# Cross-attention and mixture of experts on one core: each half of the heads on 64 array rows of its own, another order of the turn, register reads moved into the steps

## What is computed

```python
# x: (16, 112, 256), ctx: (16, 375, 256), mask: (16, 375)
q, k, v = (split_heads(layernorm(x) @ Wq.T + bq), split_heads(ctx @ Wk.T + bk), split_heads(ctx @ Wv.T + bv))
scores = where(mask == 0, -1e9, einsum('bhqd,bhkd->bhqk', q, k) / 4)
x = x + (merge(softmax(scores) @ v) @ Wo.T + bo)
flat = layernorm(x).reshape(1792, 256)
w, idx = top_k(softmax(flat @ router_w), 2);  w = w / w.sum()
h = silu(einsum('td,edf->etf', flat, w1));  y = einsum('etf,efd->etd', h, w2)
out = x + sum of w * y over the two chosen experts
```

## Time and profile before

| | us |
|---|---|
| median of 3 runs | 551.58 |
| the runs | 549.52, 551.58, 842.05 |
| the profiled execution, its own time | 552.8 |
| its span, first to last instruction | 550.6 |
| TensorE busy | 436.2 |
| VectorE busy | 349.6 |
| ScalarE busy | 261.3 |
| GpSimd busy | 191.4 |

### The profile page before, as it was taken

The page is one execution under the profiler, slowest core; times in us unless marked ns, Lnnn a source line. Parts: engine busy times, 40 slices in busy tenths (PEclk is TensorE's granted clock), DMA queues, the critical chain, the costliest instruction groups (busy, mean ns, idle before and its releaser), DMA issues.

```text
span 550.6 us, 10586 instructions
## 1 busy us (share of the span) xinstructions
PE 436.2 (79%) x4151; PEld 388.1 (70%) x4151; DVE 349.6 (63%) x743; ACT 261.3 (47%) x338; POOL 191.4 (35%) x162
## 2 busy tenths in 40 slices
PE   2557887999999999999998749322789999999810
PEld 2445666888888888888876648222689999999810
DVE  3676574777777777777773396524276667766617
ACT  3322054555565556655555204000487888788600
POOL 7371251222212222212200420002537778787420
PEclk9996698999999999999999787655699999999965
DMA  7979679899989999999634397000212222222148
GB/s 187 198 186 239 216 102 147 138 147 146 146 137 145 140 150 136 147 145 150 104 40 137 115 395 254 1 1 16 79 40 87 87 81 84 88 87 87 39 158 280
DMA packets 62624, 72.41 MB, mean 132 GB/s; under 512 B 19520, under 2 KB 57824, under 8 KB 62576
## 3 DMA queue, kind: packets, MB, share of 16 engines
q1 hardware_dynamic: 50240, 50.50, 50.7%
q0 software_dynamic: 4032, 11.02, 5.9%
q10 hardware_dynamic: 8304, 10.23, 5.3%
HBM read 37.95 MB, written 15.06 MB: 96 GB/s over the span
## 4 chain that ended last, share of the span: by engine, by line
PE 70%; DVE 11%; issue 8%; DMA 4%; ACT 3%; ACTq 2%; POOL 1%; SPq 1%; POOLq 0%; DVEq 0%
PE ps L1248 38%; PE ps L1298 10%; PE ps L1313 8%; PE ps L1327 7%; ACTq L827 2%; DMA y_back<-y_rows 2%; PE ps L1519 2%; DVE k_f L851 2%; DVE neg_max L867 1%; PE ps L1340 1%; SPq L472 1%; DVE x_rows_sb L914 1%; PE ps L1469 1%; ACT probs L667 1%; PE ps L1348 1%
## 5 line engine op out<-in xcount | busy, mean ns | idle before, releaser
L867 DVE TENSOR_REDUCE neg_max<-ps 112x1 f32<-112x376 f32 x256 | 132.9, 546 | 48.2 <-PE ps L1298 44.3
L667 ACT ACTIVATE probs<-ps 125x1344 f32<-125x1344 f32 x64 | 82.7, 1292 | 57.7 <-PE ps L1313 54.9
L1298 PE MATMUL ps<-k_stack,q_stack 98*112 98x376 f32 x256 | 89.5, 390 | 13.7 <-issue 8.6
L603 POOL DMA_INDIRECT rows<-xn_rows,token_of_row x42 | 50.2, 1195 | 76.7 <-DVE token_of_row L1125 61.5
L1298 PEld LDWEIGHTS ps<-k_stack,q_stack 98*112 98x112 f32 x256 | 42.0, 180 | 32.1 <-DVE neg_max L867 20.8
L611 POOL DMA_INDIRECT y_rows<-y_out,slot_of_row x42 | 47.9, 1140 | 33.8 <-ACT y_out L800 20.5
L502 POOL TENSOR_TENSOR k_lo<-k_f,k_hi 128x752 fp32r<-128x752 f32 x16 | 28.6, 1790 | 83.8 <-ACT k_hi L641 81.3
L493 POOL TENSOR_TENSOR ctx_lo<-ctx_raw,ctx_hi 128x752 fp32r<-128x752 f32 x16 | 28.7, 1795 | 76.9 <-ACT ctx_hi L634 76.9
L1313 PE MATMUL ps<-q_stack,k_stack 100*125 100x224 f32 x384 | 53.6, 275 | 2.1 <-ACT probs L667 1.3
L1313 PEld LDWEIGHTS ps<-q_stack,k_stack 100*125 100x125 f32 x384 | 50.1, 189 | 2.8 <-ACT probs L667 1.8
L1248 PE MATMUL ps<-w_hi,h_hi 128*128 128x256 f32 x168 | 49.0, 292 | 3.1 <-issue 1.6
(11 more groups left out here) (189 smaller groups left out, 992.4 us busy)
## 6 DMA issues: line engine op xcount, KB each, us to landing
k_stack<-k_hi SPq DMA_DIRECT2D x64, 188.0 KB, 6.4
w_all<-w ACTq DMA_DIRECT2D x16, 512.0 KB, 8.6
k_stack<-k_lo SPq DMA_DIRECT2D x32, 188.0 KB, 8.9
ctx_raw<-ctx_t SPq DMA_DIRECT2D x32, 187.5 KB, 8.7
q_stack<-q_scratch SPq DMA_DIRECT2D x32, 168.0 KB
q_scratch<-q_hi SPq DMA_DIRECT2D x16, 224.0 KB, 3.0
y_back<-y_rows SPq DMA_DIRECT2D x14, 256.0 KB, 5.4
keep<-keep_scratch SPq DMA_DIRECT2D x16, 188.0 KB, 8.9
```

The lines of the kernel that those rows point to most:

```text
L603: pool.indirect_dma_start(rows[t.ring][:, a, :], None, xn_rows, row_of(token_i, t, a))\
L667: act.activation(pf[j % 2][:, :, :], ps[0:CT, BK_ST:BK_ST + KT, 0:4 * S], ACT.Exp).then_inc(pf_ready, 1)
L867: dve.tensor_reduce(neg_max[:, s:s + 1], ps[0:S, BK_MAX + s % 2, 0:CP], AX.X, ALU.max, negate=True).then_inc(max_read, 1)
L1298: pe.matmul(ps[0:S, BK_MAX + a, 0:CP], qs[b.ring][0:R_MAX, q, S * a:S * (a + 1)], ks[b.ring][0:R_MAX, q, :], start=True, stop=True).then_i ...
```

## The change

- **Rows.** Each of the two heads of a stack gets 64 array rows of its own: head q in rows 0 to 51, head q + 8 in rows 64 to 115, each with its own mask and maximum rows. The query stack has one column block of 112 and no zeros. Every score matmul names its tile of the array: 64 rows by 128 columns, at row 0 or at row 64. A quad takes 12 matmuls of 112 columns where it took 6 of 224, alternately on the two halves, to different PSUM banks (`score_home`), with one wait on its own semaphore (`even_scored`) where the second half comes to a bank that the first half wrote.
- **Layout.** In a stack the dimension is now first and the part second: the three parts of a dimension lie in neighbouring rows, so one key transfer of 16 rows writes every third row of 48 instead of 16 neighbours. `q_scratch` is laid out likewise. The mask rows are sent twice, once per half.
- **The keep mask** (which keys count) is loaded as bytes in two transfers for all batches; it was 188 KB in each turn. The stacks' constant rows take 5 fills on GpSimd, not 8.
- **Order.** The lists of a turn on TensorE, ScalarE and VectorE are rearranged, a third home for the context's parts is added (`ctx_home`), and the key projection is cut into pieces of 3 matmuls that stand between heads 10 and 14.
- **Registers.** The reads of the expert numbers move into the steps, one per step and engine.

The diff, cut to what matters here:

```diff
-R_MASK, R_MAX, ROWS = 96, 98, 100
+HALF_ROWS = 64
+R_MASK, R_MAX, ROWS = 48, 50, 52
...
+def ctx_home(n):
+    return n if n < 2 else (0, 2, 1)[(n - 2) % 3]
+def score_home(k3, q, a):
+    at = 2 * k3 + q + 6 * a
+    return at // 4, at % 4
...
         qf = sb("q_f32", [P, KD, SG])
...
+        ch.append(sb("ctx_hi2", [P, KD, CP], F32R))
...
+        assert cursor["at"] <= queries_end, "the third context lies where the queries' low parts were"
         cursor["at"] = queries_end
...
         cursor["at"] = attn_start
...
+            def load_keep(part, batches):
+                sp.dma_start(keep[:, batches, :].rearrange("p b n -> p (b n)"),
+                             keep_scratch[batches, :].rearrange("(a b) n -> a (b n)", a=1)
+                             .to_broadcast([P, (batches.stop - batches.start) * CP])).then_inc(keep_in[part], 16)
...
-                    sp.dma_start(qs[b.ring][row:row + PARTS * DK, :, S * a:S * (a + 1)].bitcast(F32),
-                                 q_scratch[a, :, :, S * b.n:S * (b.n + 1)]
-                                 .rearrange("c (d q) n -> (c d) q n", q=HALF)).then_inc(q_stacked[b.ring], 16)
-                sp.dma_start(ks[b.ring][R_MASK:ROWS, :, :].bitcast(F32),
-                             mask_scratch[b.n:b.n + 1, :, :].rearrange("a p n -> p a n")
-                             .to_broadcast([4, HALF, CP])).then_inc(q_stacked[b.ring], 16)
+                    row = HALF_ROWS * a
+                    sp.dma_start(qs[b.ring][row:row + R_MASK, :, :].bitcast(F32),
+                                 q_scratch[a, :, :, :, S * b.n:S * (b.n + 1)].rearrange("d c q n -> (d c) q n"))\
+                        .then_inc(q_stacked[b.ring], 16)
+                    sp.dma_start(ks[b.ring][row + R_MASK:row + ROWS, :, :].bitcast(F32),
+                                 mask_scratch[b.n:b.n + 1, :, :].rearrange("a p n -> p a n")
+                                 .to_broadcast([4, HALF, CP])).then_inc(q_stacked[b.ring], 16)
...
-                        row = DK * (PARTS * a + c)
-                        sp.dma_start(ks[b.ring][row:row + DK, :, :].bitcast(F32), src[:, a, :].bitcast(F32))\
-                            .then_inc(k_stacked[b.ring], 16)
+                        row = HALF_ROWS * a
+                        sp.dma_start(ks[b.ring][row + c:row + R_MASK:PARTS, :, :].bitcast(F32),
+                                     src[:, a, :].bitcast(F32)).then_inc(k_stacked[b.ring], 16)
...
-            fills = [(qs[0][0:R_MASK, :, :], 0.0), (qs[0][R_MASK:ROWS, :, :], 1.0), (vx[0][:, :, :, DK:VC], 1.0),
-                     (qs[1][0:R_MASK, :, :], 0.0), (qs[1][R_MASK:ROWS, :, :], 1.0), (vx[1][:, :, :, DK:VC], 1.0),
-                     (qs[2][0:R_MASK, :, :], 0.0), (qs[2][R_MASK:ROWS, :, :], 1.0)]
+            fills = [(qs[0][:, :, :], 1.0), (vx[0][:, :, :, DK:VC], 1.0), (qs[1][:, :, :], 1.0),
+                     (vx[1][:, :, :, DK:VC], 1.0), (qs[2][:, :, :], 1.0)]
...
+                elif early(b, 3):
+                    act.wait_ge(vproj_done, 2)
+                elif early(b, 4):
+                    for p in range(2):
+                        act.wait_ge(q_written[p], 96 * NG // 2)
                 else:
-                    act.wait_ge(vproj_done, 2 * (b.n - 1))
-                act.copy(ch[b.par][:, :, :], c_raw[b.par][:, :, :]).then_inc(ch_ready, 1)
+                    act.wait_ge(vproj_done, 2 * (b.n - 2))
+                act.copy(ch[ctx_home(b.n)][:, :, :], c_raw[b.par][:, :, :]).then_inc(ch_ready, 1)
...
+                if has(b.after(3)):
+                    ctx_high(b.after(3))
+                if has(after):
+                    values(after, True)
                 if has(b):
                     exps(b, 0)
                 if has(after):
                     values(after, False)
-                if has(before):
-                    out_copy(before)
                 if has(b):
                     exps(b, 1)
-                if has(after):
-                    values(after, True)
-                if has(b.after(3)):
-                    ctx_high(b.after(3))
                 if has(b):
                     exps(b, 2)
                 if has(before):
...
+            experts = []
             def w1_high(t):
...
-            experts = [act.value_load(expert_of[0:1, n:n + 1], min_val=0, max_val=E - 1) for n in range(STEPS)]
...
                 if has(before):
                     normalise(before)
                 if has(after):
-                    max_rows(after)
+                    maxima(after, range(8, H))
                 if has(b.after(3)):
                     keys(b.after(3), 0)
+                if has(after):
+                    max_rows(after)
                 if has(before):
...
-            dve.wait_ge(table_ready, 1)
...
+                if KD - 1 in halves:
+                    last.then_inc(kproj_done, 1)
...
+                    else:
+                        pe.wait_ge(vx_ready, 2 * b.n)
+                elif k3 == 2:
...
                         pe.wait_ge(an_ready, b.n - 2)
...
                     a, q = s % 2, s // 2
-                    pe.matmul(ps[0:S, BK_MAX + a, 0:CP], qs[b.ring][0:R_MAX, q, S * a:S * (a + 1)],
-                              ks[b.ring][0:R_MAX, q, :], start=True, stop=True).then_inc(smax_done, 1)
+                    row = HALF_ROWS * a
+                    pe.matmul(ps[0:S, BK_MAX + a, 0:CP], qs[b.ring][row:row + R_MAX, q, :],
+                              ks[b.ring][row:row + R_MAX, q, :], start=True, stop=True, tile_position=(row, 0))\
...
-                for k3 in range(KT):
-                    for q in range(2):
-                        last = pe.matmul(ps[0:CT, BK_ST + k3, 2 * S * q:2 * S * (q + 1)],
-                                         ks[b.ring][0:ROWS, 2 * j + q, k3 * CT:(k3 + 1) * CT],
-                                         qs[b.ring][0:ROWS, 2 * j + q, :], start=True, stop=True)
+                for even, odd in zip((4, 5, 0, 1, 2, 3), (2, 3, 4, 5, 0, 1)):
+                    for a, n in enumerate((even, odd)):
+                        row, k3, q = HALF_ROWS * a, n // 2, n % 2
+                        bank, at = score_home(k3, q, a)
+                        if a == 1 and n == 0:
+                            pe.wait_ge(even_scored, QUADS * b.n + j + 1)
+                        last = pe.matmul(ps[0:CT, BK_ST + bank, S * at:S * (at + 1)],
+                                         ks[b.ring][row:row + ROWS, 2 * j + q, k3 * CT:(k3 + 1) * CT],
+                                         qs[b.ring][row:row + ROWS, 2 * j + q, :], start=True, stop=True,
+                                         tile_position=(row, 0))
+                        if a == 0 and n == 5:
+                            last.then_inc(even_scored, 1)
                 last.then_inc(st_done, 1)
...
+                def keys(t, *halves):
+                    if has(b.after(3)):
+                        project_keys(b.after(3), t, halves)
+                values(0)
                 heads(0, 1)
-                values(0)
-                heads(2)
                 outputs(before, 2)
-                heads(3, 4)
+                outputs(before, 3)
+                heads(2, 3)
+                values(2)
+                heads(4, 5)
                 scores(0)
-                heads(5)
+                heads(6)
+                if has(before):
+                    out_transpose(before)
+                heads(7)
                 values(1)
-                heads(6)
-                outputs(before, 3)
-                heads(7, 8)
+                heads(8, 9)
                 scores(1)
-                heads(9)
-                values(2)
+                outputs(b, 0)
                 heads(10)
-                outputs(b, 0)
-                heads(11, 12)
+                keys(0, 0)
+                heads(11)
+                keys(0, 1)
+                heads(12)
                 scores(2)
                 heads(13)
-                if has(before):
-                    out_transpose(before)
+                keys(1, 0)
                 heads(14, 15)
                 outputs(b, 1)
+                scores(3)
+                if has(before):
+                    attn_transpose(before)
                 if has(after):
                     max_transpose(after)
-                if has(b.after(3)):
-                    project_keys(b.after(3), 0)
-                if has(before):
-                    attn_transpose(before)
-                scores(3)
-                if has(b.after(3)):
-                    project_keys(b.after(3), 1)
+                keys(1, 1)
```

130 lines of the change are left out of this document (71 added, 59 removed).

## The result

The changed kernel takes **561.3 us** (median of 4 runs, 559.4 to 562.3) against 551.0 us, a ratio of 1.019 with an interval of 1.015 to 1.024. The forecast was 537 us, with a range of 516 to 561. It came out slower than before, though the register reads are gone from the chain.

The account below looks back on a forecast made before the run. TensorE was taken as the bound (70% of the chain), VectorE next. From the profiled 552.8 us, registers -13.6, attention turns +2 and transfers -3.5 gave 537.7, less 1.2 for the median: 537 us, range 516 to 561.

Parts of the forecast that it names:

- Registers, -13.6: Between attention and experts: 21 VectorE register reads leave the chain, -13.6 us, and cost nothing inside the steps.
- Keys before values and joined outputs, -1.30 per turn: Attention turn: -0.94 us as values no longer wait for VectorE's key read, -0.36 from fewer output blocks on column strips.
- waits for maxima: 0: Attention turn: TensorE's waits for VectorE's maxima, 0.08 us where a head follows a quad, stay about as they are: 0.
- Changes of tiling, 0.1 each: Attention turn: 14 places where TensorE goes between 64-row tiles and whole array, 0.1 us each, +1.4 per turn.
- Heads side by side, -0.15: Attention turn: two head score matmuls at once pay only for heads 0 and 1, -0.15 us, bounds 0 and -0.3.
- even_scored: Score quads: TensorE's wait for its own matmul inside every quad, 0.05 us per quad, +0.2 per turn.
- Quads, 0: Score quads: twelve matmuls of 112 columns take the 0.65 us of six of 224, as loads on both halves overlap.
- Transfers, -3.5: Start of the attention: third batch's wait for key stacks shrinks by 2.9 us, plus 0.6 for the clock; bounds 0 and -4.
- The last two turns at nothing: End of the attention: the last two turns, whose chain runs over scores and exponentials in both orders, change by nothing.
- every change costs 0.18: Rival, chance 0.2: each of 14 tiling changes per turn costs the column strips' 0.18 us, 17 us more in all, 554 us.
- Row tiles change for nothing: Rival, chance 0.27: tiling changes in the attention cost nothing, a turn is 14.0 us, 16 us below the forecast, 521 us.
- the halves load in turn: Rival, chance 0.12: weight loads of a quad's two halves do not overlap, +0.65 us per quad, 39 us, 576 us.

Follow-up runs that it names:

- before_regs: The kernel before with only the register reads of both engines moved into the experts' steps; 539.6 us, ratio 0.978.
- full_rows: The changed kernel with the scores on the whole array again instead of row tiles, all else kept; 528.4 us, ratio 0.961.
- full_early_max: full_rows with VectorE's low parts of the output and router weights moved behind the first turn's maxima; 527.9 us.
- regs_ahead: The changed kernel with its registers read in one go ahead of the steps, as before; 578.8 us in one run.
- fewer_changes: The changed kernel with 10 instead of 14 changes between row tiles and whole array per turn; 556.1 us, ratio 1.006.
- after_early_max: The changed kernel with VectorE's low parts of the output and router weights moved behind the first turn's maxima; 558.7 us, median of ten runs.
- before_tiles: regs_layout with the scores on two tiles of 64 rows, still in the old order; 573.4 us, ratio 1.038.
- extra_tile: full_rows with 8 more matmuls per turn on a 64-row tile ahead of heads, results unread; 572.8 us in one run.
- the halves in turn: The changed kernel with each quad's 6 lower-half matmuls first, then the 6 upper ones, instead of alternating; 703.7 us in one run.
- regs_layout: before_regs with the stacks' rows laid out dimension first, still whole array and old order; 536.7 us, ratio 0.970.

## Why the prediction was wrong, step by step

- **Registers, -13.6: right.** Measured -14.6 in that stage of the changed kernel, -13.9 in the same stage of before_regs, and -10 to -14 by the runs of the registers alone; the expert steps stay at 6.16 us, in the chain of the changed kernel:

```profile
447.55 0.44 PE ps L1570 x4
447.98 5.73 PE ps L1271 x48
```

- **Keys before values and joined outputs, -1.30 per turn: too much.** On the whole array the new order brings 15.00 to 14.15, -0.85. The read of the keys is gone from the chain as expected. What failed is the reading of the 0.69 us from 207.95 to 208.64 as time that comes free. In the kernel before, heads 0 and 1 stand between the last keys and the values, and TensorE runs them while VectorE reads the keys; it is idle for 0.36 us only:

```profile
207.77 0.50 PE L1298 MATMUL ps<-k_stack,q_stack 98*112 98x376 f32 x2
...
208.64 0.38 PE L1248 MATMUL ps<-attn_w_hi,ctx_hi 128*125 128x256 f32 x1 [0.36 <-DVE k_f L851]
```

In the new order the same two heads have a place of their own in the chain, 0.39 us in full_rows as in the changed kernel (220.38, above):

```profile
197.51 0.39 PE ps L1333 x2
```

So the step is worth -1.30 + 0.39 = -0.91, close to the -0.85 measured. The step "waits for maxima: 0" was right by these chains: where a head takes longer than 0.17 without a change beside it, the excess is about 0.5 us per turn in either order.
- **Changes of tiling, 0.1 each: mis-sized.** They cost 0.14 (as a mean of 16), 0.16 (four taken out) and 0.18 (beside a single head). The value was taken from a stretch of matmuls of 8 rows, where two changes were worked out as what is left of 0.83 us; no run shows that these matmuls are a tile of their own. The nearer row was the price of the column strips, 0.18. The Trainium skill, TensorEngine Tiling (Array Packing), Key Properties, says that a change of the tiling mode drains TensorE; the 0.18 us in which nothing is loaded agree with it.
- **Heads side by side, -0.15: too small.** Five pairs stand in one place per turn. One of them (heads 4 and 5) waits for a maximum and takes 0.58 us; the other four take 0.35 to 0.39 with the change ahead of them, so the second head of each is free: 4 x 0.17 = 0.7. With 14 x 0.16 = 2.2 for the changes and 1.38 measured for the row tiles as a whole, about 0.9 is given back. That these two errors nearly cancel is luck: row tiles were forecast at +1.4 + 0.2 - 0.15 = +1.45 per turn and cost 1.38. `even_scored` was not measured by itself, but a quad of 0.63 or 0.64 us against 0.65 before leaves no room for the 0.05 that it was given.
- **Quads, 0: right,** 0.64 us for twelve in the chain.
- **The steady turn** was forecast at 15.17 and measured 15.53: 0.36 x 11 = 4 us of the 24 us by which the whole was off. The 0.39 of heads 0 and 1 is about that difference.
- **Transfers, -3.5: right in its mechanism, not in its result.** The stacks land faster and the third batch's wait is gone. What follows was not foreseen: in the first turn the clock fell behind the wait of 2.48 us and stayed at its lower level until about 96 us. Instead of -3.2, the start and first two turns measured +10.5: 13.7 us of the 24.
- **"The last two turns at nothing": wrong.** They and the scores behind them cost 3.1 + 4.8 us, again at clocks of 0.88 and 0.50; with the scores on the whole array the same order had 1.00 and 0.88 there. 7.7 us of the 24. The registers' stage gave 1.4 back.

So **the clock at both ends of the attention was the missing term**: some 20 of 24 us lie in stages where the changed kernel ran at a lower granted clock than the kernel before, and no rival had it. This goes by where the time lies. One run moves the clock nearly alone: with the wait of 2.48 us taken out, the first turn fell from 27.3 to 18.3 us in the profile. The forecast looked at the earlier trace rows, a steady turn at 1.00, and took the ends of the attention to be as they were. The page of before already showed slices of 6 tenths ahead of the first turn and of 7 tenths behind the last.

Of the rivals, "every change costs 0.18" had the price right and 554 us, the nearest figure, but a turn of 16.3 that did not come. "Row tiles change for nothing" and "the halves load in turn" are refuted. The second one's condition can be seen in the quad: 0.64 us.

What stays open: why the clock falls in one run of the same kernel and not in another, and why it stays low for 22 us in which TensorE's record has no gap. The runs show only with what it goes. In the first turn, the kernels with the scores on row tiles, or with 16 additional changes, took 24 to 32 us in their profiles, except the one of 18.3 with the wait taken out; kernels without took 16.9 to 21.0. The clock falls in some of these too, after waits of 1.98 us (full_rows) and 1.64 us (full_early_max), but it is back at the full level after about 4 and 6 us, where the others stay low for 17 us and more. From the 16th transpose of the maxima to the output projection, the changed kernel, regs_ahead, fewer_changes, after_early_max and before_tiles all have 0.50, and the kernels with the scores on the whole array 0.82 to 1.00, extra_tile with its 16 additional changes among them. So there the lower clock goes with the scores on row tiles, and not with the number of changes.

## What to carry to other kernels

Count the places where TensorE goes from one tiling to another, at 0.14 to 0.18 us each in work like this, before giving small matmuls tiles of their own: here 14 of them took back more than twice what heads side by side gave, and the better kernel keeps the zeros and the whole array. Before counting a wait as time that comes free, look in the timeline for what the engine does during it: here two heads ran in it, and they had to be paid for in their new place. Price the ends of a pipeline apart from its steady state: the changed kernel's first turn takes 27.3 us at a clock of 0.56 and a steady one 15.5. Of a bundle of changes, test the parts: three of them here (registers, order, layout) bring 4% without the fourth.

## What the runs showed of the hardware

- **A change of tiling costs 0.14 to 0.18 us** at the full clock on 64-row tiles, about the 0.18 of column strips, whether the matmul has 376 columns or 64.
- **TensorE's record can be without a gap and the clock below the full one.** With the halves in turn 0.69 was granted over 270 us with 267.6 us busy; with alternating halves and the same multiplications it was 1.00 over 170.8 us. The Trainium skill, TensorE: Matmul & The Clock Gate, HAM oscillation — how this bites in real kernels, tells of a clock that falls where TensorE waits for transfers. The fall behind the 2.48 us of idle time in the first turn is of that kind, though the wait is for VectorE; the 270 us of the halves in turn have no such wait in them.
- **Rows that a transfer writes.** Every third row of 48 instead of 16 neighbours brought a low part's key stack from 9.0 to 5.1 us and a high part's from 6.4 to 4.2, in two kernels that differ in the layout alone (before_regs, regs_layout). The Trainium skill, SBUF — State Buffer, Door 1: The DMA port swizzle, has the bandwidth of a transfer depend on how many ports its partitions reach. The trace agrees in direction, with 0.57 and 0.66 of the time where the prediction worked out half.
